# Numbers of tiles' blocks packed four to a word in the edge sort, and taken out again with register operations on VectorE

## What is computed

```python
denom = jnp.maximum(deg, 1.0)[:, None]
neigh_sum = jax.ops.segment_sum(X[col], row, num_segments=n)
neigh_mean = neigh_sum / denom
H = jax.nn.relu(X @ W_root + neigh_mean @ W_neigh + b)
diffs = jnp.abs(H[row] - H[col]) ** P                       # P = 2
gg = jax.ops.segment_sum(diffs, row, num_segments=n) / denom
return jnp.tanh(gg)
```

## Time and profile before

| | us |
|---|---|
| median of three runs (3507.65 to 3513.67) | 3513.61 |
| span of the profiled execution | 3476.7 |
| sort and normalisation, to the first comparison of pass 0 | 0 to 334 |
| pass 0, first gather to last add | 326 to 1593 |
| h between the passes | 1593 to 1660 |
| pass 1 | 1660 to 2938 |
| routing and experts | 2938 to 3477 |
| busy: PE / VectorE / ScalarE / POOL | 2409.5 / 1995.0 / 881.2 / 2143.0 |

### The profile page before, as it was taken

The page is one execution under the profiler, slowest core; times in us unless marked ns, Lnnn a source line. Parts: engine busy times, 40 slices in busy tenths (PEclk is TensorE's granted clock), DMA queues, the critical chain, the costliest instruction groups (busy, mean ns, idle before and its releaser), DMA issues.

```text
span 3476.7 us, 42139 instructions
## 1 busy us (share of the span) xinstructions
PE 2409.5 (69%) x8572; PEld 1406.1 (40%) x8572; DVE 1995.0 (57%) x5224; ACT 881.2 (25%) x2525; POOL 2143.0 (62%) x2199
## 2 busy tenths in 40 slices
PE   6563565665666666658677777777777777788895
PEld 3452343343443333436222222232222222587884
DVE  8997344444444444445465666666666667666544
ACT  4695000000000000003222222222222222455442
POOL 4476666666666666667665666666666664224555
PEclk7555677677777777778788888888898889999998
DMA  0214333333333333332532333333333333333444
GB/s 26 76 4 106 92 92 94 90 93 92 92 91 92 91 92 92 91 94 85 156 93 82 93 92 93 90 94 93 90 93 96 92 94 103 115 123 122 124 136 133
DMA packets 176058, 329.74 MB, mean 95 GB/s; under 512 B 45746, under 2 KB 112510, under 8 KB 175812
## 3 DMA queue, kind: packets, MB, share of 16 engines
q0 software_dynamic: 103296, 257.55, 26.2%
q1 hardware_dynamic: 72515, 69.51, 6.2%
HBM read 284.40 MB, written 42.12 MB: 94 GB/s over the span
## 4 chain that ended last, share of the span: by engine, by line
PE 48%; DVE 16%; issue 13%; another core or an unknown queue 12%; DVEq 4%; POOL 3%; DMA 3%; ACT 1%; POOLq 0%; SPq 0%; ACTq 0%
PE ps L1125 35%; DVE big L1161 11%; PE ps L1976 6%; DVEq L1134 4%; PE ps L1950 2%; POOL edge_list L553 2%; DVE graph L1154 2%; DMA edge_list<-big 2%; PE ps L1251 1%; PE ps L1180 1%; DVEq L1161 1%; PE ps L1928 1%; DVE node L797 1%; PE ps L1182 1%
## 5 line engine op out<-in xcount | busy, mean ns | idle before, releaser
L1125 PE MATMUL ps<-arena,graph 128*128 128x258 f32 (+1 forms) x3512 | 1625.6, 612 | 809.6 <-DVE graph L1154 541.6
L1161 DVE TENSOR_TENSOR big<-ps,big 128x258 f32 (+1 forms) x1756 | 981.9, 559 | 898.5 <-remote 412.6
L1125 PEld LDWEIGHTS ps<-arena,graph 128*128 128x128 f32 x3512 | 768.9, 240 | 1659.9 <-issue 1557.3
L1091 POOL DMA_INDIRECT arena<-h_table,graph x872 | 834.7, 957 | 431.8 <-issue 218.3
L1091 POOL DMA_INDIRECT arena<-xn_table,graph x872 | 825.8, 947 | 445.3 <-issue 216.6
L1154 DVE TENSOR_SCALAR graph<-iota,graph 128x128 f32<-128x128 f32 x1756 | 531.1, 303 | 304.3 <-issue 211.2
L1106 ACT ACTIVATE arena<-arena 128x256 f32<-128x256 f32 x878 | 342.0, 412 | 916.7 <-PE ps L1125 476.7
L1189 ACT ACTIVATE late<-ps 128x256 f32<-128x256 f32 x49 | 18.8, 383 | 1075.1 <-remote 598.6
L1548 POOL DMA_INDIRECT arena<-xn_table,node x118 | 122.3, 1037 | 225.4 <-PE ps L1928 157.3
L606 PE MATMUL ps<-big,arena 128*128 128x128 f16 x832 | 98.9, 309 | 85.0 <-ACT big L643 85.0
L1976 PE MATMUL ps<-arena 128*128 128x128 f32 x944 | 130.3, 282 | 39.5 <-issue 24.9
(11 more groups left out here) (291 smaller groups left out, 1837.0 us busy)
## 6 DMA issues: line engine op xcount, KB each, us to landing
y_table<-big SPq DMA_DIRECT2D x57, 256.0 KB
arena<-xn_table,graph POOLq DMA_INDIRECT x872
arena<-h_table,graph POOLq DMA_INDIRECT x872
arena<-xn_table SPq DMA_DIRECT2D x768, 1.0 KB
arena<-h_table SPq DMA_DIRECT2D x768, 1.0 KB
xn_table<-node SPq DMA_DIRECT2D x7, 896.0 KB, 4.5
h_table<-node SPq DMA_DIRECT2D x7, 896.0 KB, 4.1
node<-in_x SPq DMA_DIRECT2D x1, 6144.0 KB
```

The source lines that it names most:

```text
L1091: e.indirect_dma_start(out=row, out_offset=None, in_=table, in_offset=bass.IndirectOffsetOnAxis(ap=idx[:, k:k + 1], axis=0)).then_inc(s_ro ...
L1125: e.matmul(out_, hot[:, k % HOTS, :], moving, start=True, stop=True).then_inc(s_sum[i], 1)
L1161: e.tensor_tensor(block, ps[a % BANKS][:, 0:width], block, ALU.add).then_inc(s_add[i], 1)
```

## The change

The sort packs the numbers of up to four blocks into one word, six bits each (49 blocks fit). `seg` is no longer multiplied by 512; VectorE adds columns 4w, 4w+1, 4w+2 and 4w+3 with the factors 1, 64, 4096 and 262144 into `seg_w` (two words per partition for seven tiles) and converts that. In the passes `dve_places` loads the two words of seven tiles, and `dve_block` takes a tile's number out of its word: a mask, and a multiplication or division by a power of two that brings it to the multiple of 512. `OFFS` stays in use for SyncE's own loads.

```diff
-            e.tensor_scalar(seg_i[:, :], seg[:, :], float(W2), None, ALU.mult).then_inc(s_seg, 1)
+            first, m = seg[:, 0:TJ:PACK], WORDS
+            for j in range(1, PACK):
+                n = len(range(j, TJ, PACK))
+                e.scalar_tensor_tensor(seg_w[:, 0:n], seg[:, j:TJ:PACK], float(1 << BITS * j), first[:, 0:n], ALU.mult,
+                                       ALU.add).then_inc(s_v, 1)
...
+                    first = seg_w
+                e.wait_ge(s_v, v.up())
+            e.tensor_copy(seg_i[:, :], seg_w[:, :]).then_inc(s_seg, 1)
@@
         def dve_places(a):
 
-            z = min(NT, a + OFFS)
-            _, places = nc.values_load_multi_w_load_instructions(
-                offs[0:1, a:z], engines=[mybir.EngineType.DVE], min_val=0, max_val=(NB - 1) * W2,
-                skip_runtime_bounds_check_because="the block's number was limited to NB - 1")
-            return dict(zip(range(a, z), places))
+            z = min(NT, a + TJ)
+            g = a // TJ * WORDS
+            _, words = nc.values_load_multi_w_load_instructions(
+                offs[0:1, g:g + WORDS], engines=[mybir.EngineType.DVE], min_val=0, max_val=(1 << BITS * PACK) - 1,
+                skip_runtime_bounds_check_because="four numbers of blocks, each limited to NB - 1")
+            return {k: (words[(k - a) // PACK], (k - a) % PACK) for k in range(a, z)}
+
+        def dve_block(place, a):
+
+            word, j = place.pop(a)
+            bits, up = word & ((1 << BITS) - 1 << BITS * j), W2.bit_length() - 1 - BITS * j
+            return nc.s_assert_within(bits << up if up >= 0 else bits >> -up, 0, (NB - 1) * W2,
+                                      skip_runtime_bounds_check_because="a block's number was limited to NB - 1")
@@
-                if a >= 0 and a % OFFS == 0 and a + OFFS < NT:
-                    place.update(dve_places(a + OFFS))
+                if a >= 0 and a % TJ == 0 and a + TJ < NT:
+                    place.update(dve_places(a + TJ))
@@
-                    block = acc[:, bass.ds(place.pop(a), width)]
+                    block = acc[:, bass.ds(dve_block(place, a), width)]
```

More of the change, by code:

```diff
@@ L21 @@
 OFFS = 8
+PACK, BITS = 4, 6
 TOP_PAD = 8
@@ L63, in gnn_moe_kernel @@
     TJ = -(-NT // P)
+    WORDS = -(-TJ // PACK)
+    assert NB <= 1 << BITS and PACK * BITS <= 24
     W1 = D + 2
     W2 = 2 * D
+    assert W2 & (W2 - 1) == 0
     CODE = 256
@@ L100, in gnn_moe_kernel @@
         edge_list = nc.dram_tensor("edge_list", [SPARE_ROW + CC * GG * P, R8], F32, kind="Internal").ap()
-        block_of = nc.dram_tensor("block_of", [1, P * TJ], I32, kind="Internal").ap()
+        block_of = nc.dram_tensor("block_of", [1, P * WORDS], I32, kind="Internal").ap()
         sp_list = nc.dram_tensor("sp_list", [SPT, P], U32, kind="Internal").ap()
@@ L162, in gnn_moe_kernel @@
         assert SLOTS * D <= SLOTS * W1 + 2 * D - LISTS * P and (RING + 2) * W1 <= SLOTS * D
-        offs = graph[0:1, HOTS * P + NT + NTR:HOTS * P + NT + NTR + P * TJ].bitcast(I32)
+        offs = graph[0:1, HOTS * P + NT + NTR:HOTS * P + NT + NTR + P * WORDS].bitcast(I32)
         iota = sb("iota", [P, P])
@@ L177, in gnn_moe_kernel @@
         block_two = sb("block_two", [P, NB, 2], F16)
-        seg_i = sb("seg_i", [P, TJ], I32)
+        seg_w = sb("seg_w", [P, WORDS])
+        seg_i = sb("seg_i", [P, WORDS], I32)
         stats = sb("stats", [P, NB, 6])
@@ L886, in dve_edges @@
             e.wait_ge(s_v, v.up())
-            e.tensor_scalar(seg_i[:, :], seg[:, :], float(W2), None, ALU.mult).then_inc(s_seg, 1)
+            first, m = seg[:, 0:TJ:PACK], WORDS
[3 more added lines that the diff above has]
+                                       ALU.add).then_inc(s_v, 1)
+                if j == 1:
+                    if n < m:
+                        e.tensor_copy(seg_w[:, n:m], first[:, n:m]).then_inc(s_v, 1)
+                        v.up()
+                    first = seg_w
+                e.wait_ge(s_v, v.up())
+            e.tensor_copy(seg_i[:, :], seg_w[:, :]).then_inc(s_seg, 1)
         def dve_list(e, c):
```

## The result

| on the same chip | median us of the runs | lowest to highest | runs |
|---|---|---|---|
| before | 3513.48 | 3503.76 to 3522.18 | 13 |
| after | 3523.16 | 3515.99 to 3529.95 | 13 |

After takes 1.0033 times as long (95% interval 1.0023 to 1.0043): 0.33 %, or some 10 us, slower. The prediction was 3432 us, 82 us faster, with a range of 3360 to 3520 us. The sign is wrong and the time lies 3 us above the range. What happened looks like rival 2: the loads' time went, and the passes got no shorter.

A forecast was written before the change was run, and what follows sets the result against it. The prediction took PE and VectorE, not POOL, to pace the two passes. Loads gain 166 us, register operations lose 84: 82 us off 3513.6 gives 3432 us, range 3360 to 3520 us.

The forecast's parts named there:

- rival 2: Passes: saved load time goes into waits the loads had hidden; 110 us gained, 101 lost, 3505 us; chance 0.10.
- PE and VectorE, who hand each other selection matrices and sums,: Both passes: these two engines set the pace, at 1.44 and 1.46 us per tile.
- POOL is not what paces a pass: Both passes: gathers need 1.27 us per tile, 1107 us a pass; POOL waits another 425 us for ring slots.
- The loads' share: VectorE's register loads in the passes: 0.6 of 276 us is on the path, 166 us gained (110 to 276).
- The register operations' share: Ahead of each tile's add: 0.5 of 169 us is on the path, 84 us lost (56 to 169).
- both low ends: Lower shares on the path, from the chain of waits: loads 0.4, register operations 0.33.
- The prices: VectorE's sequencer: two-register load 518 ns, register operation 28, third fused step 18, division as any step; 96 ns per tile.
- the sum: Both passes: 166 us of loads less 84 us of register operations, 82 us gained; both shares high, 107 us.
- the distances of 2.12 us in undisturbed stretches: Passes: adds stand that far apart where a load stands between two tiles, otherwise 0.63 us in pass 0.
- The sort: Before the passes: three more small VectorE operations of about 0.2 us, covered by a wait for PE; nothing, 0.6 us uncovered.
- 37 us that the change does not touch: Whole kernel: difference between profiled span 3476.7 us and median 3513.6 us, carried unchanged into the forecast.
- Rival 1: Ahead of each add: register operations or divisions are slow and cost more than the loads saved; 3556 us; chance 0.12.

The follow-up runs named there:

- e1: After with its two-register loads but no register operation, so sums go to wrong blocks; 1.0015 of before.
- e8: Before with one more VectorE comparison (128x120, about 0.28 us) per tile into an unread spare tile; 1.0022 of before, 8 us slower.
- e9: Before with GpSimd's gathers replaced by plain transfers of the table's first 128 rows; 2623.6 us, 0.7463 of before.
- e10: After with GpSimd's gathers replaced by plain transfers of the table's first 128 rows; 2527.7 us, 0.7182 of before.
- e14: Before with the gathers using 12 of the ring's 16 slots; 0.9981 of before.
- e13: Before with gathers bringing only 64 of 128 rows from the 17th tile of each pass on; 0.9999 of before.
- e2: Before with one register operation (a mask changing nothing) more per tile, behind the waits; 1.0025 of before.
- e16: e5 with 2 instead of 6 SyncE tiles per pass and 12 of 16 ring slots for gathers; 3484.5 us, 0.9945 of before.
- e17: e16 with the change of this study (packed numbers, register operations); 0.9973 of before.
- e5: Before with the wait for a tile's sum on the add itself, one VectorE semaphore instruction fewer per tile; 0.9985 of before, 5 us faster.
- e12: After with the sum's wait on the add itself, register operations ahead of it, one VectorE semaphore instruction fewer per tile; 1.0007 of before.
- e3: After with mask and shift done into an own register ahead of the comparison, one sequencer instruction more per tile; 1.0163 of before.
- e4: Before, unpacked, with a load of two registers for every two tiles instead of eight for eight; 1.0021 of before.
- e6: Before with gathers bringing 512 instead of 1024 bytes of a row from the 17th tile of each pass on; 0.9993 of before.
- e7: Before with each of SyncE's tiles brought by one plain transfer instead of 128 row transfers; 0.9929 of before, 25 us faster.

## Why the prediction was wrong, point by point

**The failed step** is that "PE and VectorE, who hand each other selection matrices and sums," pace a pass, as far as it takes the length of VectorE's own work for the pace, and with it the shares of 0.6 and 0.5 that it sets on that. What the runs showed: e1 took 276 us of VectorE's waiting away and gained nothing, e8 put each tile's add 0.11 us later in undisturbed stretches and cost 8 us of 193. Only with plain transfers in place of gathers was VectorE's time on the path (e9 and e10, 96 us).

The other half of the sentence, "POOL is not what paces a pass", can't be called wrong. The rows lay in the ring for some 15 us before TensorE started on them (e14). But it can't be called right either, for a pass keeps close to what GpSimd does. Worked out from the gathers' starts, a gather starts 1.25 us after the last one, 1090 us for 872. Some 110 to 130 times a pass it starts later than that, 165 us in all (163 and 166 in e8, where VectorE was busy 257 us longer; 178 and 183 in after; 170 and 179 with the ring of 12; 203 and 212 in e13, beside its shorter step). With plain transfers both parts went. So it is shown that the gathers in flight hold a pass at this length, and that neither VectorE's work, the bytes, the rows nor the ring's depth does. Whether they do it by their own step of 1.25 us, by what they do to the sequencers and semaphores of the others, or by the two in turn, is not shown. Plain transfers spaced 1.25 us apart would tell; they weren't run.

**The shares.** The loads' share, 0.6 with a low end of 0.4, was nearer to 0: e1 removed them without a gain. The register operations' share was not 0.5 either: e8, a delay of their size per tile, costs 8 us of 193, a share of 0.04. The chain of waits, on which both low ends rested, gave VectorE's sequencer 5.9 % and 3.8 % of the passes. It is a path through the records, which takes each wait for its last releaser; it doesn't tell what would be late next. Here it was TensorE's sum, which the prediction names as late next, without a time for it: 1160 us of waiting ahead of after's adds.

**The prices** hold in the main, the register operation's least: a load 527 ns (518), the register operation 40 (28), a fused step 24 more (18), a divided one 44 more (priced as any), adds 0.74 and 0.98 us apart (0.73 and 0.99), a load's remaining cost in pass 0 0.15 us (0.17), idle ahead of comparisons 38 us (about 20). e9 and e10 confirm the sum: 96 us where the gathers don't cover it. The prediction's objection to rival 2, the distances of 2.12 us in undisturbed stretches, was true and beside the point. In those stretches VectorE works off tiles at 0.63 us where gathers start every 1.25 us, so they can't make up a whole pass. Made quicker, they were followed by as much more waiting (e1: 83 us less and 83 us more in pass 0).

**What made after slower rather than equal** has no cause that is shown, only a rule of thumb from these runs: one more instruction per tile in VectorE's queue costs 0.2 to 0.3 %. It was 0.33 % in after, 0.25 in e2, 0.22 in e8 (a comparison, no register operation), 0.28 from e16 to e17 and 0.22 from e5 to e12. One fewer gave 0.15 % (e5) and 0.26 (from after to e12). The slow instructions that after's third sequencer instruction brings (446 in after, 314 in e2, 949 in e3) are not shown to be the cause: e17 loses as much to e16 without any. e3, with the most, does lose the most. One rival stays untested. The loss may go by the length of the program, of which the prediction took no account for want of a row: after has 1791 instructions more than before, e2 and e8 have 1756, and lose 8 to 12 us; but e1 loses 5 us with 35 more, and e3 57 us with 3547. The sort, where the prediction put nothing, has a part in it as far as single traces tell: in the six traces of kernels with the new sort the first gather starts at 327.2 to 330.0 us (mean 328.8), in the thirteen others at 324.0 to 327.7 us (mean 325.6), so some 3 us are lost before the first tile. Why e1 and e4 are 0.15 and 0.21 % slower than before is otherwise not explained.

**The sum against the runs.** The "37 us that the change does not touch" between the span and the median were no part of the program. A run's time is its span and some 2 us, here and in all 17 experiments (3484.5 and 3481.9 us in e16, for instance); the profiled execution of before, whose time by this was some 3479 us, was a faster one, and series on other chips had medians from 3478 to 3518 us for the same kernel.

**Rivals.** Rival 2 gave 3505 us, 9 us faster where after is 10 us slower; its mechanism, stops that would take the time anyway, is the one that held, with a load share of 0 where it took 0.4. It should have had most of the chance. Rival 1's mark, adds over 0.8 us apart in undisturbed stretches, did not appear; a fused operation with a division takes 90 ns against 70.

**What stays open.** Why sequencer instructions take 0.70 us while gathers are in flight, what keeps a pass at the same length when VectorE's part of it shrinks or grows, and what makes the 165 us of long steps. The runs exclude bytes (e6), rows (e13), ring depth (e14), VectorE's load (e8) and, for the most part, SyncE's rows (e7, 0.7 %). Gathers fewer in number, each for more than one tile, weren't tried.

## What to carry to other kernels

Don't look for the pace in busy and idle time alone: for an engine that does one kind of work in a stage they add up to the stage whoever paces it (e9). Look at how long a result lies before it is used: here rows lay 15 us, and sums that were done lay 6 us and more before VectorE heard of them. Test for slack with one cheap run that adds work (e8) before you remove any: 257 us added for 8 us of time says that little removed there can gain. And trade no long load for more short instructions on a sequencer unless it paces: here 276 us of loads were worth nothing, and one more instruction per tile cost 0.2 to 0.3 %.

## What the runs showed of the hardware

- With gathers in flight, register, move and issue instructions of SyncE take up to 0.70 us and its double in place of 0.03 to 0.23, in stretches; so do register and semaphore instructions of VectorE in the runs with three or more of them per tile (after, e2, e3). VectorE's add keeps its 0.43 us there. With plain transfers of the same bytes (e9, e10) none of these did. In before, e12 and e17, with two per tile, none of VectorE's did.
- In such a stretch of before, the semaphore raises for four finished sums came together, over 6 us after the matmuls' recorded ends.
- A gather of 128 rows by GpSimd takes 0.95 us and starts every 1.25 us, with 512 or 1024 bytes a row; its rows of 1 KB have landed 1.46 us after its end. 64 rows take 0.91 us. A plain transfer of the same 128 KB takes 0.54 us of GpSimd.
- A register load on VectorE is 527 ns for two registers and 1844 for eight. A register operation takes 40 ns, a fused one 46, 70 or 90 ns (two steps, three, three with a division).
- TensorE's granted clock was 0.72 and 0.85 in the passes with gathers, where it was busy 61 and 75 % of the time, and 0.97 and 1.00, at or near the upper of its two levels, in those of e9, where it was busy 81 and 87 %.
